# Normalisation ahead of the spread stage: ScalarE scales and writes four of the eight tokens of a tile, VectorE the other four

## The chip, the cores and the metric

The kernel runs on one core of a Trainium2 chip. Its time is the device time of one launch in microseconds (us), lower is better. The profiled execution has its own time, and the profile counts its times from the start of the span that it recorded.

## What is computed

The program is four blocks of an image network on an input of 4 images, 64 channels, 128 x 128 pixels. The change touches only the start of the last convolution-like block (L3): a normalisation over the 64 channels of every pixel, whose result goes into repeated rolls and 3 x 3 depthwise filters.

```python
def _ln_c(v, eps=1e-06):
    m = jnp.mean(v, axis=1, keepdims=True)
    s = jnp.var(v, axis=1, keepdims=True)
    return (v - m) / jnp.sqrt(s + eps)
...
def _L3_conv_ref(x, w_d, w_u, w_r, w_l, bn_d, bn_u, bn_r, bn_l):
    ...
    for w, bn, dil, sign, axis in dirs:
        dim = H if axis == 2 else W
        for i in range(ITER):
            shift = dim // 2 ** (ITER - i)
            idx = (np.arange(dim) + sign * shift) % dim
            xs = x[:, :, idx, :] if axis == 2 else x[:, :, :, idx]
            x = x + ALPHA * jax.nn.relu(_aspp(xs, w[i], bn[i], dil))
    return x
...
x = x + _L3_conv_ref(_ln_c(x), ...)
```

## The kernel before

The stages run one after the other (window attention, a choice layer, a convolution, a top-2 layer, sweeps, a choice layer, spread, a top-2 layer), each with its own semaphores, and every stage ends in a barrier of all engines. `stage_spread` is the one that changes. It has two phases: the normalisation, and then 8 groups of 16 filter steps on TensorE, ScalarE and VectorE. TensorE, ScalarE and VectorE wait for the last tile of the normalisation (L2678, L2656, L2605) before the first filter step, so nothing of the second phase lies beside the first except the building of filter bands on GpSimd and their loads.

A tile of the normalisation is 128 partitions (image rows) x 8 tokens (pixels of a row) x 64 channels, 512 elements in each partition. There are 16 positions t times 4 images b, 64 tiles. For tile n the steps are:

- SP loads the tile into `xs` (L2469), four buffers deep, each load after GpSimd has read the buffer's last tile.
- VectorE sums the channels (`total`, L2587) and divides by 64 (`mean`, L2591).
- GpSimd subtracts the mean into `h` (`center`, L2518), four buffers deep. It waits for the mean, and for the scaled tile four back.
- ScalarE squares `h` (`square`, L2648), VectorE sums the squares (`variance`, L2595), ScalarE takes the root (`root`, L2653).
- VectorE inverts the root (L2600) and multiplies `h` by it into `passes` (`scale`, L2602). `passes` is the array [128, 64 channels, 4 images, 128 columns], so that consecutive channels of one token are written 512 floats (2048 bytes) apart, while `h` is read without gaps. `passes` is read by the filter steps alone.

`pipelined` sets the order on each engine: every step has a lead d, and in step v of the loop the engine does, one after the other, each function for tile v + d. VectorE's list is `[(total, 3), (variance, 1), (mean, 3), (scale, 0)]`, ScalarE's `[(root, 1), (square, 2)]`, GpSimd's `[(center, 3)]`. In VectorE's step v stand the total of tile v + 3, the variance of tile v + 1, the mean of tile v + 3, and the inverse and the scaling of tile v. The loop body holds four steps, with three steps of filling ahead and the last ones written out after it. A counter is raised by 4 at the start where four buffers are free from the beginning (L2510, L2511).

Of the kernel before, what the change touches and what calls it, by code (L numbers as in the profile page):

```python
# [6 lines left out]
ALU = mybir.AluOpType  # L7
ACT = mybir.ActivationFunctionType
AX = mybir.AxisListType
B, C, H, W = 4, 64, 128, 128  # L10
# [64 lines left out]
def bcast(v, n, m=C):  # L75

    return v.unsqueeze(2).to_broadcast([128, n, m])


def pipelined(eng, tiles, stages):  # L80

    def step(v):
        for f, d in stages:
            if 0 <= v + d < B * tiles:
                f((v + d) // B, (v + d) % B, v + d)

    for v in range(-max(d for _, d in stages), B):
        step(v)  # L90
    with eng.Fori(1, tiles - 1) as t:
        for k in range(B):
            for f, d in stages:
                f(t + (k + d) // B, (k + d) % B, B * t + k + d)
    for v in range(B * (tiles - 1), B * tiles - min(d for _, d in stages)):
        step(v)
# [2229 lines left out]
def stage_spread(nc, tok, w_d, w_dirs, bns, y, windows):  # L2326
# [9 lines left out]
    TS = 8  # L2336
    NT = W // TS
# [9 lines left out]
    with ExitStack() as ctx:  # L2347
        a = Arena(nc, ctx, "sp")
# [7 lines left out]
        st = a.sb("st", [128, B, 2, TS])  # L2356

        xs = work[:, 0:2048].rearrange("p (n t c) -> p n t c", n=B, t=TS)
        h = work[:, 2048:4096].rearrange("p (n t c) -> p n t c", n=B, t=TS)
# [23 lines left out]
        inverted = a.sem("inverted")  # L2383
# [2 lines left out]
        var_ready = a.sem("var_ready")  # L2386
        std_ready = a.sem("std_ready")
        y_ready = a.sem("y_ready")
        band_in = [a.sem(f"band_in{i}") for i in range(LOADS)]
        band_ready = a.sem("band_ready")  # L2390
        y_done = a.sem("y_done")
# [12 lines left out]
        def columns(n, b, t):  # L2404

            v = y[:, :, bass.ds(b, 1), bass.ds(TS * t, TS)]
            return v.rearrange("p c a w -> p (a w) c")

        def channel(g, q):
            return y[:, NC * g + q, :, :].rearrange("p b w -> p (b w)")  # L2410

        def place(i, q):

            return x[:, (q, q, 8 + q if q < 4 else q - 4, 4 + q)[i // IT], :]
# [19 lines left out]
        def loads_before(slot, j):  # L2434

            return 16 * sum(2 * len(row_parts(k)) for k in range(j) if k % LOADS == slot)
# [54 lines left out]
        @block.gpsimd  # L2491
        def _(pool):
            link = Link(pool, pool_done)

            pool.memset(eps[:, 0:1], EPS_LN)
            pool.memset(eps[:, 1:2], EPS_BN)
            pool.memset(bands[0:C + 1, :], 0.0).then_inc(vs_clear, 1)
            link(pool.memset(roll[:, :, :], 0.0))

            def set_diagonal(m, c0, c1, k):  # L2500

                link(pool.affine_select(out=m[:, c0:c1], in_=m[:, c0:c1], compare_op=ALU.not_equal, fill=1.0,
                                        base=-c0 - k, pattern=[[-1, c1 - c0]], channel_multiplier=1))

            for i, s in enumerate(SHIFTS):
                for c0 in (0, R):
                    set_diagonal(roll[:, i, :], c0, c0 + R - s // 2, s // 2)
                    set_diagonal(roll[:, i, :], c0 + R - s // 2, c0 + R, s // 2 - R)
            pool.sem_inc(const_ready, 1)
            pool.sem_inc(centered, 4)  # L2510
            pool.sem_inc(y_ready, 4)  # L2511
            pool.sem_inc(var_ready, 2)

            def center(t, b, n):

                pool.wait_ge(mean_ready, n + 1)
                pool.wait_ge(y_ready, n + 1)
                pool.tensor_tensor(h[:, b, :, :], xs[:, b, :, :], bcast(st[:, b, 0, :], TS),  # L2518
                                   ALU.subtract).then_inc(centered, 1)

            pipelined(pool, NT, [(center, 3)])

            def turn_over(g, j):

                pool.wait_ge(band_in[j % LOADS], g * loads_before(j % LOADS, NV) + loads_before(j % LOADS, j + 1))
                last = NV * g + j - BANDS
                if last >= 0:
                    for q in range(NC - 4, NC):
                        pool.wait_ge(conv_ready[q], 2 * (ITS * (last // NV) + IT + last % NV + 1))
                src = hankel[:, j % LOADS, :].rearrange("p (q n) -> p q n", q=NC)[:, :, 0:3 * R]  # L2530
                dst = band[:, (NV * g + j) % BANDS, :, :, :].rearrange("p q k m -> p q (k m)")
                pool.tensor_copy(dst, src[:, :, ::-1]).then_inc(band_ready, 1)  # L2532

            def put_back(g, q):


                pool.wait_ge(x_ready[q], ITS * (g + 1))
                src = place(ITS - 1, q).rearrange("p (b s m k) -> p s b m k", b=B, s=2, m=8)
                dst = channel(g, q).rearrange("p (b m s k) -> p s b m k", b=B, s=2, m=8)
                for here in range(2):  # L2540
                    for there in range(2):
                        ins = pool.tensor_copy(dst[halves[there], here], src[halves[here], there])
                        if here == 0 or there == 0:
                            link(ins)
                ins.then_inc(y_done, 1)
                pool.wait_ge(y_done, NC * g + q + 1)

            for j in range(BANDS):
                turn_over(0, j)
            for g in range(GROUPS):  # L2550
                for j in range(BANDS, NV):
                    turn_over(g, j)
                for q in range(NC):
                    put_back(g, q)
                    if g < GROUPS - 1 and q in (3, 5, 7):
                        turn_over(g + 1, (q - 3) // 2)

        @block.vector
        def _(dve):
# [3 lines left out]
            for d in range(3):  # L2563
                dil = (1, 2, 4)[d]
                for kh in range(3):
# [3 lines left out]
                    ins = dve.tensor_copy(vs[0:C, d, 0:IT, 3, at], w[:, 0:IT, 0])  # L2569
# [22 lines left out]

            def variance(t, b, n):
                dve.wait_ge(squared, n + 1)
                dve.tensor_reduce(st[:, b, 1, :], sq[:, b % 2, :, :], AX.X, ALU.add).then_inc(var_ready, 1)  # L2595

            def scale(t, b, n):
                s = st[:, b, 1, :]
                dve.wait_ge(std_ready, n + 1)
                dve.reciprocal(s, s).then_inc(inverted, 1)  # L2600
                dve.wait_ge(inverted, n + 1)
                dve.tensor_tensor(columns(n, b, t), h[:, b, :, :], bcast(s, TS), ALU.mult).then_inc(y_ready, 1)  # L2602

            pipelined(dve, NT, [(total, 3), (variance, 1), (mean, 3), (scale, 0)])
            dve.wait_ge(y_ready, B * NT + 4)  # L2605

            def add(g, i, q):
                old, new = x_before(g, i, q), place(min(i + 1, ITS - 1), q)
# [29 lines left out]
        @block.scalar  # L2638
        def _(act):
            act.wait_ge(const_ready, 1)  # L2640
            act.wait_ge(p_in, 16 * 5)
            var = raw_bn[:, :, :, 3, :]
            act.activation(var, var, ACT.Sqrt, bias=eps[:, 1:2]).then_inc(bn_std, 1)

            def square(t, b, n):
                act.wait_ge(centered, n + 5)
                act.wait_ge(var_ready, n + 1)
                act.activation(sq[:, b % 2, :, :], h[:, b, :, :], ACT.Square).then_inc(squared, 1)  # L2648

            def root(t, b, n):  # L2650
                s = st[:, b, 1, :]
                act.wait_ge(var_ready, n + 3)
                act.activation(s, s, ACT.Sqrt, bias=eps[:, 0:1], scale=1.0 / C).then_inc(std_ready, 1)  # L2653

            pipelined(act, NT, [(root, 1), (square, 2)])
            act.wait_ge(y_ready, B * NT + 4)  # L2656
            act.wait_ge(par_ready, 1)

            def relu(g, i, q, out, rows_out, rows_in):
                c = NC * g + q  # L2660
                return act.activation(out[rows_out, :], pC[q][rows_in, :], ACT.Relu, bias=par[rows_in, c, BI + i:BI + i + 1],  # L2661
                                      scale=par[rows_in, c, SC + i:SC + i + 1])

            for g in range(GROUPS):
                for i in range(ITS):
                    for q in range(NC):
                        act.wait_ge(conv_ready[q], 2 * (ITS * g + i + 1))
                        if aside(i, q):
                            relu(g, i, q, side[:, q // 4, :], halves[0], halves[1])
                            ins = relu(g, i, q, side[:, q // 4, :], halves[1], halves[0])  # L2670
                        else:
                            ins = relu(g, i, q, pC[q], slice(0, 128), slice(0, 128))
                        ins.then_inc(relu_ready[q], 1)

        @block.tensor
        def _(pe):
            pe.wait_ge(const_ready, 1)
            pe.wait_ge(y_ready, B * NT + 4)  # L2678


            MINUS, MIDDLE, PLUS = range(3)
# [98 lines left out]
```

## Time and profile before

| what | value |
|---|---|
| median of 3 runs | 7505.19 us (7491.1 to 7510.78) |
| the profiled execution's own time | 7501.84 us |
| its span | 7500.1 us |
| granted TensorE clock, mean of the span | 0.853 |
| VectorE busy, all stages | 4316.2 us (58%) |
| ScalarE busy, all stages | 3784.3 us (50%) |
| GpSimd busy, all stages | 1430.9 us (19%) |
| first operation of the normalisation phase | 5012.44 us |
| first matmul after it | 5215.08 us |

The last two rows bound the phase: 203 of 7500 us. The shares of the whole span say little about it, as the other stages have other limits. It has to be read from a timeline of its own stretch, from the durations of its lines, and from what its engines wait for.

### The profile page before, as it was taken

The numbers are of one execution on the slowest core, as the hardware profiler recorded it, in microseconds if no ns is written. First come the engines' busy times: TensorE is split into PE (matmuls) and PEld (weight loads), VectorE is DVE, ScalarE is ACT, GpSimd is POOL, SyncE is SP. The second block draws the span as 40 slices with busy tenths as digits, with TensorE's granted clock in tenths as the row PEclk, the third lists the DMA queues.
The fourth block names the chain that finished last, engine by engine and source line by source line (L and its number), as shares of the span: only waits on it lengthen the run. The fifth ranks groups of instructions, "written<-read, shape, count | busy, mean of one in ns | idle before, by whom it ended". The sixth has DMA issues, their size and how long they took to land. (4 is left out here: it accounts for less than half of the span.)

```text
span 7500.1 us, 128640 instructions
## 1 busy us (share of the span) xinstructions
PE 5733.5 (76%) x43616; PEld 3796.3 (51%) x43616; DVE 4316.2 (58%) x8974; ACT 3784.3 (50%) x7044; POOL 1430.9 (19%) x1334
## 2 busy tenths in 40 slices
PE   6776777666697777669979997541999999566666
PEld 4555556315354333359979994240555555332222
DVE  5665666563622777772223345538777777565565
ACT  5665666542643666462233323403666676454453
POOL 2332333432421000050000002312111121111110
PEclk9888888875698888869989998755999999777778
DMA  0101000121232767530000022214666676256666
GB/s 25 29 23 29 21 26 23 57 68 34 84 87 86 241 233 232 199 91 0 0 0 0 34 101 86 62 51 89 82 84 86 75 85 80 40 178 176 178 178 189
DMA packets 791912, 645.40 MB, mean 86 GB/s; under 512 B 494273, under 2 KB 641921, under 8 KB 791501
## 3 DMA queue, kind: packets, MB, share of 16 engines
q1 hardware_dynamic: 790477, 639.00, 35.0%
q8 instruction: 241, 3.95, 0.2%
q14 instruction: 170, 1.39, 0.1%
q0 software_dynamic: 1024, 1.05, 0.1%
HBM read 549.73 MB, written 90.20 MB: 85 GB/s over the span
## 5 line engine op out<-in xcount | busy, mean ns | idle before, releaser
L2300 PE MATMUL sw_pC<-sw_row,sw_wc 128*128 128x128 f32 x10160 | 1159.2, 274 | 56.8 <-DVE sw_row L2175 54.9
L2300 PEld LDWEIGHTS sw_pC<-sw_row,sw_wc 128*128 128x128 f32 x10160 | 1148.6, 191 | 58.1 <-DVE sw_row L2175 55.5
L2721 PE MATMUL sp_pC<-sp_work,sp_bands 64*64 64x512 f32 (+11 forms) x14592 | 986.1, 428 | 44.7 <-issue 44.7
L2721 PEld LDWEIGHTS sp_pC<-sp_work,sp_bands 64*64 64x64 f32 x14592 | 596.3, 133 | 437.8 <-issue 369.5
L2163 DVE SCALAR_TENSOR_TENSOR sw_row<-sw_pC,sw_y 128x128 f32<-128x128 f32 x1016 | 337.8, 332 | 792.7 <-PE sw_pC L2300 792.7
L2661 ACT ACTIVATE sp_pC<-sp_pC,sp_par 128x512 f32<-128x512 f32 x832 | 597.7, 740 | 375.5 <-PE sp_pC L2721 349.6
L1715 DVE TENSOR_TENSOR t_z<-t_z,t_ht 128x1024 f32<-128x1024 f32 x512 | 601.9, 1233 | 150.2 <-DMA t_z<-gate_rows 149.3
L1874 PE MATMUL t_pO<-t_z,t_ew 128*64 128x512 f32 x2048 | 557.5, 690 | 36.4 <-DVE t_z L1715 35.8
L2232 ACT ACTIVATE sw_y<-sw_row 128x128 f32 (+1 forms) x762 | 265.3, 348 | 593.6 <-DVE sw_row L2163 593.6
L2624 DVE TENSOR_TENSOR sp_work<-sp_work,sp_pC 128x512 f32<-128x512 f32 x512 | 351.0, 687 | 171.2 <-ACT sp_pC L2661 170.7
L1844 PE MATMUL t_pT<-t_ident,t_h 128*128 128x128 f32 x1024 | 195.8, 354 | 274.3 <-ACT t_gs L1771 157.9
L309 POOL TENSOR_TENSOR wa_sc<-wa_sc,wa_sm 128x1024 f32<-128x1024 f32 x128 | 243.3, 1901 | 712.0 <-DVE wa_sm L406 712.0
L1005 PE MATMUL c_pG<-c_ht,c_gate_cols 128*32 128x512 f32 x512 | 291.0, 703 | 80.7 <-ACT c_ht L950 80.7
L579 PE MATMUL wa_pS<-wa_ks,wa_qs 128*128 128x256 f32 x1024 | 322.2, 470 | 23.2 <-issue 18.3
L1874 PEld LDWEIGHTS t_pO<-t_z,t_ew 128*64 128x64 f32 x2048 | 153.0, 159 | 361.0 <-issue 263.1
L1844 PEld LDWEIGHTS t_pT<-t_ident,t_h 128*128 128x128 f32 x1024 | 156.2, 183 | 340.0 <-issue 275.8
L1780 ACT ACTIVATE t_oc<-t_pO 128x512 f32<-128x512 f32 x128 | 76.6, 599 | 497.4 <-PE t_pO L1874 497.4
L579 PEld LDWEIGHTS wa_pS<-wa_ks,wa_qs 128*128 128x128 f32 x1024 | 246.3, 244 | 110.1 <-issue 64.6
L2661 ACT ACTIVATE sp_side<-sp_pC,sp_par 64x512 f32<-64x512 f32 x384 | 297.0, 773 | 7.5
L2532 POOL COPY sp_bands<-sp_bands 128x1536 f32<-128x1536 f32 x96 | 141.4, 1473 | 815.0 <-PE sp_pC L2721 778.0
L393 DVE TENSOR_TENSOR wa_sc<-wa_pS,wa_bias 128x1024 f32<-128x1024 f32 (+1 forms) x128 | 147.8, 1155 | 252.9 <-PE wa_pS L579 250.2
L455 ACT ACTIVATE wa_qs<-wa_pQK,wa_gmask 128x256 f32<-128x256 f32 x256 | 107.3, 470 | 363.4 <-PE wa_pV L572 363.4
(346 smaller groups left out, 10834.3 us busy)
## 6 DMA issues: line engine op xcount, KB each, us to landing
t_z<-gate_rows SPq DMA_DIRECT2D x512, 512.0 KB, 6.7
sp_bands<-windows SPq DMA_DIRECT2D x128, 512.0 KB
c_xs<-tokens SPq DMA_DIRECT2D x128, 256.0 KB, 2.6
cb_xs<-tokens SPq DMA_DIRECT2D x128, 256.0 KB, 2.8
wa_xs<-in_x SPq DMA_DIRECT2D x64, 256.0 KB, 2.9
tokens<-wa_xt SPq DMA_DIRECT2D x128, 128.0 KB, 2.1
tokens<-cb_h SPq DMA_DIRECT2D x64, 256.0 KB, 2.4
t_xs<-tokens SPq DMA_DIRECT2D x32, 512.0 KB, 9.3
```

What stands on the lines that cost most here:

```text
L309: pool.tensor_tensor(p, p, r, ALU.mult).then_inc(probs_ready, 1)
L579: ins = pe.matmul(pS[:, w, :, :], qs[:, w, :, :].rearrange("p g q -> p (g q)"), ks[:, :, 64 * w:64 * w + 64], start=True, stop=True)
L1005: ins = pe.matmul(pG[m][E * b:E * b + E, :], gate_cols[:, m, :], ht[:, b % 2, :], start=True, stop=True)
L1715: dve.tensor_tensor(z[:, i, q, :], z[:, i, q, :], ht[:, m.k % HR, i, :], ALU.mult).then_inc(z_ready, 1)
L1844: ins = pe.transpose(pT[s][:, 128 * j:128 * j + 128], h[:, i, 4 * s + j, :, :].rearrange("p c d -> p (c d)"), ident[:, :])
L1874: ins = pe.matmul(pO[i][64 * s:64 * s + 64, :], ew[:, q, :], z[:, i, q, 512 * s:512 * s + 512], start=(q == 0), stop=(q == 3))
L2163: dve.scalar_tensor_tensor(row[par][c][:, :, PAD:PAD + P2], pC[c][:, 0:2 * P2].rearrange("p (b w) -> p b w", b=2), 0.0, line(sweep, c, i), ...
L2232: act.activation(line(sweep, c, i), row[par][c][:, :, PAD:PAD + P2], ACT.Copy).then_inc(saved[c], 1)
L2300: ins = pe.matmul(pC[c][:, 0:2 * P2], wc[:, sweep, m, :], row[1 - par][c][:, :, m:m + P2], start=(m == 0), stop=(m == 4))
L2624: return dve.tensor_tensor(new, old, rel, ALU.add)
L2661: return act.activation(out[rows_out, :], pC[q][rows_in, :], ACT.Relu, bias=par[rows_in, c, BI + i:BI + i + 1], scale=par[rows_in, c, SC + ...
L2721: ins = pe.matmul(out[halves[to], :, low * lo:low * hi], band[halves[k], (NV * g + j) % BANDS, q, AT[k][tap], :], v[halves[k], :, low * at ...
```

## The change

ScalarE gets a third function in its list, `scale_rest` with lead 0, behind `root` and `square`: after VectorE's inverse of tile n it multiplies tokens 4 to 7 of tile n by their inverse, one ACTIVATE (Copy with a scale read from `st`, one value in each partition) for each token, 128 x 64 elements, and writes them into `passes`. VectorE's multiplication now covers tokens 0 to 3. A new semaphore `rest_ready` counts tiles whose second half is written: GpSimd waits for it before it writes `h` again, VectorE before it writes the variance again (`st` is read by ScalarE until then), and TensorE and VectorE wait for the last tile's second half before the filter steps.

```diff
@@ stage_spread, GpSimd @@
+            pool.sem_inc(rest_ready, 4)
...
                 pool.wait_ge(mean_ready, n + 1)
                 pool.wait_ge(y_ready, n + 1)
+                pool.wait_ge(rest_ready, n + 1)
                 pool.tensor_tensor(h[:, b, :, :], xs[:, b, :, :], bcast(st[:, b, 0, :], TS),
@@ VectorE @@
             def variance(t, b, n):
                 dve.wait_ge(squared, n + 1)
+                dve.wait_ge(rest_ready, n + 1)
...
-                dve.tensor_tensor(columns(n, b, t), h[:, b, :, :], bcast(s, TS), ALU.mult).then_inc(y_ready, 1)
+                dve.tensor_tensor(columns(n, b, t)[:, 0:TS // 2, :], h[:, b, 0:TS // 2, :], bcast(s[:, 0:TS // 2], TS // 2),
+                                  ALU.mult).then_inc(y_ready, 1)
...
             dve.wait_ge(y_ready, B * NT + 4)
+            dve.wait_ge(rest_ready, B * NT + 4)
@@ ScalarE @@
-            pipelined(act, NT, [(root, 1), (square, 2)])
+            def scale_rest(t, b, n):
+                act.wait_ge(inverted, n + 1)
+                for k in range(TS // 2, TS):
+                    ins = act.activation(columns(n, b, t)[:, k, :], h[:, b, k, :], ACT.Copy, scale=st[:, b, 1, k:k + 1])
+                ins.then_inc(rest_ready, 1)
+
+            pipelined(act, NT, [(root, 1), (square, 2), (scale_rest, 0)])
@@ TensorE @@
             pe.wait_ge(y_ready, B * NT + 4)
+            pe.wait_ge(rest_ready, B * NT + 4)
```

How the order on ScalarE changes, at the first step of the loop body. Before (ISA and REGISTER_ALU rows work out addresses and counts):

```order
L91 ISA
L2653 ACTIVATE sp_st<-sp_st,sp_eps 128x8
L2646 REGISTER_ALU
L2647 REGISTER_ALU
L2648 ACTIVATE sp_work<-sp_work 128x512
```

The changed kernel's ScalarE at the same place (L2659 is the root, L2654 the square, L2664 the new line):

```order
L91 ISA
L2659 ACTIVATE sp_st<-sp_st,sp_eps 128x8
L2652 REGISTER_ALU
L2653 REGISTER_ALU
L2654 ACTIVATE sp_work<-sp_work 128x512
L2662 REGISTER_ALU
L2664 ISA
L2664 ACTIVATE passes<-sp_work,sp_st 128x64
L2664 ISA
L2664 ACTIVATE passes<-sp_work,sp_st 128x64
```

Two more such pairs follow for the last two tokens; then comes the next step's root. No table load stands between them. VectorE before, from the variance of the first step in the loop body to its scaling:

```order
L2595 TENSOR_REDUCE sp_st<-sp_work 128x8
L2590 REGISTER_ALU
L2591 TENSOR_SCALAR sp_st<-sp_st 128x8
L2599 REGISTER_ALU
L2600 RECIPROCAL sp_st<-sp_st 128x8
L2602 ISA
L2602 TENSOR_TENSOR passes<-sp_work,sp_st 128x8x64
```

VectorE of the changed kernel at the same place:

```order
L2599 TENSOR_REDUCE sp_st<-sp_work 128x8
L2593 REGISTER_ALU
L2594 TENSOR_SCALAR sp_st<-sp_st 128x8
L2603 REGISTER_ALU
L2604 RECIPROCAL sp_st<-sp_st 128x8
L2606 ISA
L2606 TENSOR_TENSOR passes<-sp_work,sp_st 128x4x64
```

The rows and their order stay; the multiplication has half the elements.

## Rows read from the trace of the kernel before

**Rows 1.** The page: span, and busy time of each engine.
```profile
span 7500.1 us, 128640 instructions
PE 5733.5 (76%) x43616; PEld 3796.3 (51%) x43616; DVE 4316.2 (58%) x8974; ACT 3784.3 (50%) x7044; POOL 1430.9 (19%) x1334
```

**Rows 2.** Waits of TensorE: who waited for whom, us in total, times, longest.
```profile
PE sp_pC L2734 <- DVE passes L2602: 246.2, 1, 246.2
```

**Rows 3.** Groups by line, 5016.0 to 5209.3: busy us, mean ns | idle before.
```profile
L2602 DVE TENSOR_TENSOR passes<-sp_work,sp_st 128x512 f32 (+1 forms) x61 | 107.3, 1758 | 8.2
...
L2653 ACT ACTIVATE sp_st<-sp_st,sp_eps 128x8 f32<-128x8 f32 x62 | 18.7, 301 | 142.9 <-DVE sp_st L2595 142.9
```

**Rows 4.** Timeline of one step: start us, us, engine, line, operation [idle before].
```profile
5103.10 0.15 DVE L2591 TENSOR_SCALAR sp_st<-sp_st 128x8 f32<-128x8 f32 x1
5103.17 0.19 DVE L2600 RECIPROCAL sp_st<-sp_st 128x8 f32<-128x8 f32 x1
5103.21 0.30 ACT L2653 ACTIVATE sp_st<-sp_st,sp_eps 128x8 f32<-128x8 f32 x1 [2.36 <-DVE sp_st L2595]
5103.33 1.04 POOL L2518 TENSOR_TENSOR sp_work<-sp_work,sp_st 128x512 f32<-128x512 f32 x1 [2.13 <-DVE sp_st L2591]
5103.42 0.61 ACT L2648 ACTIVATE sp_work<-sp_work 128x512 f32<-128x512 f32 x1
5103.50 1.75 DVE L2602 TENSOR_TENSOR passes<-sp_work,sp_st 128x512 f32 x1
...
5105.10 0.66 DVE L2587 TENSOR_REDUCE sp_st<-sp_work 128x8 f32<-128x512 f32 x1
...
5106.28 0.15 DVE L2591 TENSOR_SCALAR sp_st<-sp_st 128x8 f32<-128x8 f32 x1
```

**Rows 5.** Durations of three lines: ns min/median/max, first and last start.
```profile
L2602 DVE TENSOR_TENSOR passes<-sp_work,sp_st x64: 1011/1749/1861, 5017.6 to 5213.9; 128x512 f32 x56, 128x512 f32<-128x512 f32 x8
...
L878 DVE TENSOR_TENSOR c_h<-c_h,c_st x64: 691/1528/1566, 1413.5 to 4801.2; 128x512 f32<-128x512 f32 x64
...
L1653 DVE TENSOR_TENSOR t_rw<-t_rw,t_z x2: 167/168/169, 2409.1 to 6494.5; 128x8 f32<-128x8 f32 x2
```

**Rows 6.** Timeline of another stage's normalisation.
```profile
4602.64 1.04 POOL L830 TENSOR_TENSOR c_h<-c_xs,c_st 128x512 f32<-128x512 f32 x1 [4.20 <-DVE c_st L866]
4602.70 1.53 DVE L878 TENSOR_TENSOR c_h<-c_h,c_st 128x512 f32<-128x512 f32 x1
```

**Rows 7.** Timeline of the end of the phase.
```profile
5210.86 0.61 ACT L2648 ACTIVATE sp_work<-sp_work 128x512 f32<-128x512 f32 x1
5212.05 0.66 DVE L2595 TENSOR_REDUCE sp_st<-sp_work 128x8 f32<-128x512 f32 x1
...
5213.92 1.01 DVE L2602 TENSOR_TENSOR passes<-sp_work,sp_st 128x512 f32<-128x512 f32 x1
```

**Rows 8.** Durations of ScalarE lines in other stages, as in rows 5.
```profile
L1347 ACT ACTIVATE cb_xb<-cb_zero x8: 239/240/240, 1997.5 to 2376.0; 128x64 f32<-128x64 f32 x8
...
L1787 ACT ACTIVATE t_y<-t_pY x64: 576/578/599, 2470.7 to 3144.9; 128x512 f32<-128x512 f32 x64
L1787 ACT ACTIVATE passes<-t_pY x64: 1009/1016/1074, 6590.7 to 7479.1; 128x512 f32 x48, 128x512 f32<-128x512 f32 x16
...
L1753 ACT ACTIVATE t_h<-passes,t_nm,t_sd x512: 451/484/508, 6520.4 to 7435.0; 128x126 f32 x128, 128x126 f32<-128x126 f32 x43
```

**Rows 9.** Timeline of ScalarE: eight activations of L1753 in a row.
```profile
6623.25 3.15 ACT L1753 ACTIVATE t_h<-passes,t_nm,t_sd 128x126 f32 x8
```

**Rows 10.** Timeline: ScalarE writes `passes`, and VectorE beside it.
```profile
6622.43 1.02 ACT L1787 ACTIVATE passes<-t_pY 128x512 f32<-128x512 f32 x1
...
6623.03 0.23 DVE L1705 TENSOR_TENSOR t_one<-t_one,t_ex 128x128 f32<-128x128 f32 x1
```

**Rows 11.** SP's loads of tiles: issue ns, and time to landing.
```profile
L2469 SPq DMA_DIRECT2D sp_work<-tokens x128: 598/607/1927, 4998.4 to 5197.5; - x128
...
DMA to landing us min/median/max: 2.6/2.8/6.4
```

More of the change, by code:

```diff
@@ L2388, in stage_spread @@
         y_ready = a.sem("y_ready")
+        rest_ready = a.sem("rest_ready")
         band_in = [a.sem(f"band_in{i}") for i in range(LOADS)]
```

## The prediction

> **What bounds the kernel now.** I read the page first, for where the stage lies: the engines' shares over all stages [rows 1] say nothing about a phase of 203 us. What matters for it is TensorE's waits: its longest single one, 246.2 us, ends with the last write of `passes` by L2602 [rows 2]. So the whole second phase stands behind the normalisation, and a microsecond saved there should come off the total one for one, if the filter steps then take what they take now.
>
> Next the groups by line in the steady part [rows 3]. In 193.3 us VectorE's L2602 alone is busy 107.3 us with only 8.2 us of idle ahead of it, while ScalarE sat 142.9 us waiting for the variance. VectorE is the engine without a gap. The timeline of one step shows why it is [rows 4]: the mean starts at 5103.10, the next step's at 5106.28, a pitch of 3.18 us, and between them VectorE does the inverse, the scaling (1.75 us), and then the total at 5105.10, 0.15 us before the scaling's recorded end.
>
> The 1.75 us is not the price of 512 elements. The same line takes 1.01 us at its shortest [rows 5], at the very end of the phase [rows 7], where center is over. In the step, GpSimd's center runs from 5103.33 to 5104.37, starting 0.17 us ahead of the scaling, and the scaling ends at 5105.25, 0.88 us after it [rows 4]. VectorE does next to nothing of it until GpSimd is through. Another stage has the same picture with a write without gaps: center ends at 4603.68, the multiplication at 4604.23, 0.55 us later [rows 6], where free it takes 0.69 us [rows 5]. The Trainium skill (SBUF — State Buffer, "Who interferes with whom") says that a VectorE instruction with two SBUF inputs contends with a GpSimd instruction that reads SBUF, as an exclusive lock for the whole instruction. By that rule the trace agrees: 1.75 us beside center, 1.01 us without.
>
> **The change part by part.**
>
> *Half of the scaling leaves VectorE.* Only the tail behind center shrinks; the locked 0.87 us stays. The tail is 0.88 us for 512 elements into strided places and 0.55 us into places without gaps; the difference, 0.33 us, grows with the elements, and so do most of the 0.55 us: a multiplication of 8 elements takes 168 ns and one of 512 takes 691 [rows 5], 1.04 ns an element, so 512 elements are 0.53 of the 0.55. The tail is then about 0.015 + 512 x 1.68 ns, and 256 elements leave 0.445 us. Saved: 0.43 us a step. Bounds: a tail wholly in proportion gives 0.44; if the 0.14 us by which a free one is longer than its tail (1.01 - 0.88) also stands in the tail, half is 0.51 and the step saves 0.37. I take 0.43, since the small multiplication places the fixed part outside the tail. What is late next is the same chain, center then the shorter tail: 5104.37 + 0.445 - 0.15 puts the next total at 5104.67 instead of 5105.10, a pitch of 2.75 us.
>
> The step with the tail occurs 61 times: L2602 from its first start at 5017.6 to the end of the steady part at 5209.3 [rows 3, 5]. 61 x 0.43 = 26.2 us.
>
> *Four activations go to ScalarE.* No row shows a 128 x 64 activation with a scale pointer into strided places. Lower bound: 0.24 us, a plain 128 x 64 copy; upper bound 0.48 us, 126 elements with a bias and a scale pointer [rows 8]. In between: 0.24, plus 64 x (1016 - 578)/512 ns = 0.055 for the stride, plus a pointer. The 484 ns of L1753 are 240 + 62 elements at some 0.8 ns + two pointers, so about 0.097 each. That is 0.39 us. Eight L1753 in a row take 3.15 us [rows 9], (3.15 - 0.48)/7 = 0.38 apart where each lasts 0.48, so neighbours overlap by 0.10; the pitch P of the new ones is 0.29, and of the bounds 0.14 and 0.38. The register work between them is inside L1753's pitch as well. The Trainium skill (ScalarE: Activation LUTs, "What ACT_TABLE_LOAD costs") prices an ACTIVATE at 186 ns + 0.833 ns an element, 93 ns for a pointer, with 93 ns of overlap: an estimate from that page is 0.33 us without the stride, a pitch of 0.24, and the sum below would be the same by it.
>
> ScalarE's step is then root 0.21 + square 0.52 (starts at 5103.21 and 5103.42, its 0.61 less the overlap) + 4 x 0.29 = 1.9 us, against a pitch of 2.75. With the upper P it is 2.25. It starts with the variance and ends at about 5105.2, before the next root at 5105.96 and before the next center at 5106.08, the first that waits for it. Cost on the path: nothing. The cover is VectorE's pitch, and it is gone at P = 0.50.
>
> *The new waits.* Center's on `rest_ready`: 0.9 us of slack as worked out, with nothing queued behind on GpSimd but the next center. The variance's on `rest_ready`: for a tile three steps back, long done; the sequencer meets it while the total runs, and behind it are the variance, the mean and the scaling. I price both at nothing; no row shows such a wait by itself, and the nearest step, 0.07 us from one short instruction to the next [rows 4], would give 61 x 0.07 = 4.3 us as the upper bound. Below nothing there is no room: a wait does no work.
>
> *Loads.* SP needs two issues of 0.61 us a tile and 2.8 us to landing [rows 11]; from the end of center to the total four steps on there are 4 x 2.75 - 2.4 = 8.6 us. No cost.
>
> *The end of the phase.* Here the gain is not had. VectorE's last three scalings would end 1.3 us earlier against the steady part. But ScalarE must still write three halves: its square ends at 5211.47 [rows 7], the first four follow until 5212.6; the root of the last tile (variance at 5212.05, 0.43 sooner, done by 5212.3) until 5212.8; four until 5213.9; four more until 5215.2 with the last one's full length. Now the last scaling ends at 5214.93. So the end is 0.25 us later than now, on top of the 26.2.
>
> **Sum.** 26.2 - 0.25 = 26.0 us. Against the profiled execution's own 7501.84 (span 7500.1) that gives 7475.9. That execution is 3.35 us under the median of the runs, so I forecast for the median 7505.19 - 26.0 = 7479.2, as **7479 us**, a gain of 0.35%. The likeliest case's own size runs from 61 x 0.37 - 0.25 = 22.3, or 18 with the upper price of the waits, to 61 x 0.44 = 26.8 us; the three runs lie 20 us apart, so 7467 to 7491.
>
> **The rivals.**
>
> *Two strided writers get in each other's way, gain gone.* In the new step VectorE's tail (5104.37 to 5104.81) lies in the middle of ScalarE's writes (5103.9 to 5105.2) into the same array. If each then runs at half speed, the tail of 0.445 doubles to 0.89 and VectorE's pitch is what it is now: 7505. Against it: ScalarE writes `passes` for 1.02 us while L1705, a two-input VectorE instruction, takes its usual 0.23 us [rows 10]; but that one writes without gaps, so it doesn't settle it. For it: both engines pay for the stride by a like amount (0.6 and 0.86 ns an element), which could be one limit at the memory. The skill's SBUF page, in the section named above, says that ScalarE never waits on anyone for SBUF; no run here shows two strided writers together.
>
> *ScalarE becomes the bound, slower than before.* The same collision, felt by ScalarE. Its step is 0.73 + 4P; at P = 0.50 it takes over from VectorE, and from P = 0.61 the step is longer than today's 3.18. If each of the four lasts twice its 0.39, P is 0.68 and the step 3.45: 61 x 0.27 = 16 us slower, 7522. Center, the variance and the root would all wait for it. Against it: even the dearest short row has P = 0.38.
>
> *The tail does not shrink.* If the 0.88 us were mostly a handing over after GpSimd, and not elements, half the elements would save little: 7505. Against it: the tails of 0.88 and 0.55 for equal counts differ exactly as the free durations do.
>
> **How the numbers follow.** About 0.3% (22.5 us) is what a measurement of this kernel tells from no change. Main case 0.76; collision with the gain gone or mostly gone 0.12; ScalarE as the bound 0.05; tail that stays 0.07. Of the main case about seven tenths come out beyond 22.5 us (forecast 26, sizes down to 18, and medians that move by some us), the rest within. Faster: 0.76 x 0.71 + 0.01 = 0.55. Slower: 0.05 and a little for drawn runs, 0.06. Same: 0.39. The range reaches from a little under the main case's lower end, 7465, to the no-gain cases at 7505; outside stay the slower case and the tails of the runs.
>
> **What would show it.** Right: L2602's successor (L2606) at 1.25 to 1.35 us in the steady part, its end 0.43 to 0.46 after center's; pitch of the means 2.75; L2664 near 0.39 us; TensorE's wait shorter by 26 us; ScalarE still waiting for the variance, some 0.85 us a step. Wrong: a tail of 0.6 us or more (collision, or a fixed part); L2664 over 0.6 us; center waiting for ScalarE instead of for the mean; or a phase shorter by 26 us and a total that is not, which would put the loss into the filter steps or the top-2 stage behind them.

## The result, and the profile after

The changed kernel takes 7472.21 us (median of 8 runs, 7463.21 to 7491.64), the kernel before 7502.62 us (median of 8, 7491.1 to 7511.44). The ratio is 0.9963 with a 95% interval of 0.9950 to 0.9975, a gain of 28 us (19 to 38); the two medians themselves lie 30.4 us apart. The forecast was 7479 us and a gain of 26.0 us, 0.35%, with a range of 7465 to 7505: the time lies inside it, and the interval of the gain holds the forecast. The gain is just over the 0.3% that the prediction called measurable, so the totals alone would not tell 26 us from 20 or from 35.

The wait in which TensorE stands before the filter steps shows the change without the noise of the other stages. It was 246.2 us [rows 2]. Now (waits of TensorE: who waited for whom, us in total, times, longest):

```profile
PE sp_pC L2747 <- ACT passes L2664: 220.1, 1, 220.1
```

That is 26.1 us less, where 26.0 was forecast, and the releaser is now ScalarE's last activation instead of VectorE's last multiplication, as the forecast's end of the phase had it.

The groups by line in the steady part of the changed kernel, against [rows 3] (busy us, mean ns | idle before):

```profile
L2606 DVE TENSOR_TENSOR passes<-sp_work,sp_st 128x256 f32 (+1 forms) x61 | 81.1, 1330 | 8.2
L2664 ACT ACTIVATE passes<-sp_work,sp_st 128x64 f32 (+1 forms) x243 | 67.0, 387 | 0.0
...
L2659 ACT ACTIVATE sp_st<-sp_st,sp_eps 128x8 f32<-128x8 f32 x61 | 18.3, 301 | 55.9 <-DVE sp_st L2599 55.9
```

VectorE's multiplication went from 1.76 to 1.33 us on the mean, though it has half the elements. ScalarE took 67 us of new work and still waits 55.9 us for the variance, in place of 142.9. One step of the timeline, against [rows 4]:

```profile
5103.14 0.16 DVE L2594 TENSOR_SCALAR sp_st<-sp_st 128x8 f32<-128x8 f32 x1
5103.21 0.19 DVE L2604 RECIPROCAL sp_st<-sp_st 128x8 f32<-128x8 f32 x1
5103.25 0.30 ACT L2659 ACTIVATE sp_st<-sp_st,sp_eps 128x8 f32<-128x8 f32 x1 [0.92 <-DVE sp_st L2599]
5103.37 1.04 POOL L2521 TENSOR_TENSOR sp_work<-sp_work,sp_st 128x512 f32<-128x512 f32 x1 [1.71 <-DVE sp_st L2594]
5103.46 0.61 ACT L2654 ACTIVATE sp_work<-sp_work 128x512 f32<-128x512 f32 x1
5103.54 1.32 DVE L2606 TENSOR_TENSOR passes<-sp_work,sp_st 128x256 f32 x1
5103.98 1.10 ACT L2664 ACTIVATE passes<-sp_work,sp_st 128x64 f32 x4
5104.71 0.66 DVE L2590 TENSOR_REDUCE sp_st<-sp_work 128x8 f32<-128x512 f32 x1
...
5105.89 0.16 DVE L2594 TENSOR_SCALAR sp_st<-sp_st 128x8 f32<-128x8 f32 x1
```

The means are 2.75 us apart (3.18 before). Center ends at 5104.41 and the multiplication at 5104.86, 0.45 us later (0.88 before). The first 0.87 us of the multiplication, beside center, are still there: they are two thirds of VectorE's instruction. ScalarE's four activations end at 5105.08, well before the next root at 5106.00.

The end of the phase in the changed kernel, against [rows 7]:

```profile
5200.11 1.46 POOL L2535 COPY sp_bands<-sp_bands 128x1536 f32<-128x1536 f32 x1 [2.25 <-DMA sp_bands<-windows]
...
5200.53 1.49 DVE L2606 TENSOR_TENSOR passes<-sp_work,sp_st 128x256 f32<-128x256 f32 x1
5200.72 1.11 ACT L2664 ACTIVATE passes<-sp_work,sp_st 128x64 f32<-128x64 f32 x4
5201.86 0.18 DVE L2604 RECIPROCAL sp_st<-sp_st 128x8 f32<-128x8 f32 x1
5202.08 0.59 DVE L2606 TENSOR_TENSOR passes<-sp_work,sp_st 128x256 f32<-128x256 f32 x1
5202.08 1.12 ACT L2664 ACTIVATE passes<-sp_work,sp_st 128x64 f32<-128x64 f32 x4 [0.25 <-DVE sp_st L2604]
```

The last tile's activations end at 5203.20, 0.5 us after VectorE's last one. The size came out as forecast, but not all of the way there: the band copy on GpSimd, which now waits for its load, falls on VectorE's multiplication of the last tile but one (1.49 us where free it takes 0.59; in the kernel before it fell one tile earlier, on a multiplication of 1.44 us where free it takes 1.01), and ScalarE waits 0.25 us for the last inverse. The forecast had ScalarE busy without a gap there.

The two profiled executions differ by 19.6 us of span (7500.1 and 7480.5), which is not the phase's 26.1. TensorE's first matmul after the wait starts at 5215.08 in one and 5203.34 in the other, 11.7 us earlier, so the stages ahead of the phase, whose code is the same, took 14.4 us longer in the second execution; what follows the phase took 7.9 us less. Single executions scatter by that much, so a change of this size is better read in its own wait than in one total.

### The profile page after: what moved, and what is told of

Same layout as the page of the kernel before. It is cut to its first block and busy times, and to the rows that moved or that the text cites. A ratio compares the mean times of both kernels' runs of the same rounds, so it can differ in the third digit from the quotient of the medians.

```text
span 7480.5 us, 129214 instructions
## 1 busy us (share of the span) xinstructions
PE 5739.0 (77%) x43616; PEld 3804.1 (51%) x43616; DVE 4287.6 (57%) x8974; ACT 3848.5 (51%) x7300; POOL 1433.9 (19%) x1334
```

## Experiments

Each kernel ran beside the kernel before on the same chip. Of each I read two things: the ratio of the times, and TensorE's wait, which carries the phase without the rest.

### The tail by the number of elements: VectorE six tokens, or two

```diff
-                dve.tensor_tensor(columns(n, b, t)[:, 0:TS // 2, :], h[:, b, 0:TS // 2, :], bcast(s[:, 0:TS // 2], TS // 2),
+                dve.tensor_tensor(columns(n, b, t)[:, 0:6, :], h[:, b, 0:6, :], bcast(s[:, 0:6], 6),
...
-                for k in range(TS // 2, TS):
+                for k in range(6, TS):
```

> VectorE scales tokens 0 to 5 of a tile, ScalarE 6 and 7. Elements theory (the tail behind center is 0.015 us + 1.68 ns an element): the 384 elements of VectorE leave a tail of 0.66 us, the scaling lasts 1.53 to 1.55 us, the step is 2.96 us, TensorE's wait is 246.2 - 61 x 0.215 = 233 us, the ratio to the kernel before 0.998. Fixed-part theory (0.14 us of the tail belongs to the handing over): the half's 0.445 us then would not lie on this line, and 384 elements leave 0.69 us or more, a step of 3.0 us. Collision theory (two strided writers slow each other): fewer strided writes on ScalarE, so the tail is shorter than 0.66 us.

Measured: 7498.59 against 7509.36 us, ratio 0.9984 (0.9975 to 0.9994). TensorE's wait and one step:

```profile
PE sp_pC L2747 <- DVE passes L2606: 232.6, 1, 232.6
```
```profile
5093.36 1.04 POOL L2521 TENSOR_TENSOR sp_work<-sp_work,sp_st 128x512 f32<-128x512 f32 x1 [1.92 <-DVE sp_st L2594]
...
5093.53 1.54 DVE L2606 TENSOR_TENSOR passes<-sp_work,sp_st 128x384 f32 x1
```

Center ends at 5094.40, the multiplication at 5095.07: a tail of 0.67 (0.66 as the median of the 61). The step is 2.96 us as forecast, and TensorE's wait 232.6 us for 233.

The same edit with 2 for 6:

> VectorE scales tokens 0 and 1 of a tile, ScalarE 2 to 7. Elements theory: a tail of 0.23 us for 128 elements, a step of 2.53 us; ScalarE's step is 0.73 + 6 x 0.24 = 2.2 us and stays below it, so VectorE still bounds. TensorE's wait is 220.1 - 61 x 0.215 = 207 us, plus 1 to 2 us at the end of the phase, where ScalarE writes the last three tiles' six tokens after one another: 208 to 209. The ratio to the kernel before is 0.995. Fixed-part theory: a tail of 0.30 us or more and a wait of 213 us. Collision theory: ScalarE's strided writes now cover the whole tail and the step, its activations last over 0.45 us, and the step is 2.75 us or more.

Measured: 7473.67 against 7509.36 us, ratio 0.9942 (0.9924 to 0.9961).

```profile
PE sp_pC L2747 <- ACT passes L2664: 208.6, 1, 208.6
```
```profile
5091.49 1.04 POOL L2521 TENSOR_TENSOR sp_work<-sp_work,sp_st 128x512 f32<-128x512 f32 x1 [1.49 <-DVE sp_st L2594]
...
5091.66 1.14 DVE L2606 TENSOR_TENSOR passes<-sp_work,sp_st 128x128 f32 x1
```

The four tails, medians over 61 steps, are 0.875 us for 512 elements, 0.66 for 384, 0.447 for 256 and 0.266 for 128. The first three lie on a line of 1.67 ns an element with 0.02 us left at zero; the last is 0.04 longer than the line, but the step is not (2.536 us for 2.53). The third rival of the prediction, a tail that does not shrink, is out. So is the collision of two strided writers in the size that the prediction gave it, a tail or an activation of twice the length: in the changed kernel ScalarE's activations cover the whole tail, and it lies on the line. Here, with six activations, ScalarE writes for 1.6 of every 2.5 us, and the step is as short as elements alone make it (durations of ScalarE's activations in ns min/median/max, in the changed kernel and in this one).

```profile
L2664 ACT ACTIVATE passes<-sp_work,sp_st x256: 383/387/402, 5032.5 to 5202.8; 128x64 f32 x112, 128x64 f32<-128x64 f32 x16
```
```profile
L2664 ACT ACTIVATE passes<-sp_work,sp_st x332: 383/387/427, 5039.7 to 5179.5; 128x64 f32 x165, 128x64 f32<-128x64 f32 x1
```

In the changed kernel the activation lasts 387 ns whether it meets VectorE's tail or not. In this one the maximum is 427, and it is no stray: the second of the six activations, the one for token 3, lasts over 395 ns in 60 of 64 tiles (0.423 us as a median), the other five last 387.

```profile
5092.33 0.42 ACT L2664 ACTIVATE passes<-sp_work,sp_st 128x64 f32 x1
```

It lies across VectorE's tail (5092.53 to 5092.80), and its 0.036 us are the size of what that tail has too much. So there is a small collision here, and it costs nothing, as the step shows. The rule that the prediction took from the Trainium skill (SBUF — State Buffer, "Who interferes with whom"), that ScalarE never waits on anyone, agrees with the 387 ns of the changed kernel, but not with these 423, and here the measurement decides. What makes the difference is not shown; the last section says what these activations have in common.

### ScalarE's part alone

VectorE multiplies all eight tokens; ScalarE makes its four activations as well, into a scratch buffer without gaps.

```diff
+        flat = a.sb("flat", [128, B, TS // 2, C])
...
-                dve.tensor_tensor(columns(n, b, t)[:, 0:TS // 2, :], h[:, b, 0:TS // 2, :], bcast(s[:, 0:TS // 2], TS // 2),
-                                  ALU.mult).then_inc(y_ready, 1)
+                dve.tensor_tensor(columns(n, b, t), h[:, b, :, :], bcast(s, TS), ALU.mult).then_inc(y_ready, 1)
...
+                act.wait_ge(rest_ready, n + 1)
                 for k in range(TS // 2, TS):
-                    ins = act.activation(columns(n, b, t)[:, k, :], h[:, b, k, :], ACT.Copy, scale=st[:, b, 1, k:k + 1])
+                    ins = act.activation(flat[:, b, k - TS // 2, :], h[:, b, k, :], ACT.Copy, scale=st[:, b, 1, k:k + 1])
```

> Only ScalarE's part of the change: VectorE multiplies all eight tokens as before, and ScalarE makes its four activations all the same, with the new waits, but into a scratch buffer without gaps that nobody reads. Hidden theory (the four activations and the waits cost nothing while VectorE's step is the longer one): step 3.18 us, scaling 1.75 us, TensorE's wait 246 to 247 us, ratio 1.000; the activations last about 0.33 us, and their pitch shows whether the stride costs time between them (0.24 us with it in the changed kernel). Waits theory: up to 0.07 us a step, TensorE's wait 250 us.

Measured: 7508.17 against 7509.36 us, ratio 1.0002 (0.9993 to 1.0012).

```profile
PE sp_pC L2748 <- ACT sp_flat L2665: 246.7, 1, 246.7
```
```profile
L2665 ACT ACTIVATE sp_flat<-sp_work,sp_st x177: 331/332/335, 5039.8 to 5179.8; 128x64 f32<-128x64 f32 x177
```

The activations and all the new waits together cost 0.5 us on the phase, some 0.3 of it over the 61 steps and the rest at the end. The step is 3.183 us on the mean, 3.178 in the kernel before. The waits theory's 250 us is out. The activation lasts 332 ns without the stride and 387 with it, but starts follow each other after 0.24 us in both: the stride costs time in an activation, not time between activations.

### The lock: the scaling ahead of the mean

The kernel before, with one list reordered. Nothing goes to ScalarE.

```diff
-            pipelined(dve, NT, [(total, 3), (variance, 1), (mean, 3), (scale, 0)])
+            pipelined(dve, NT, [(total, 3), (variance, 1), (scale, 0), (mean, 3)])
```

> The kernel before with one edit: in VectorE's list the scaling stands ahead of the mean, so that center, which waits for the mean, starts after the scaling and runs beside the total and the variance, which have one input from SBUF. ScalarE has no part of the scaling. Lock theory (the 0.74 us between 1.75 and 1.01 is time in which GpSimd's center keeps VectorE's two-input instruction out): the scaling lasts 1.01 us, the step is 0.58 + 0.60 + 0.33 + 0.86 + 0.07 = 2.44 us, TensorE's wait 246.2 - 61 x 0.74 = 201 us, the ratio 0.994. Rival (the scaling is slow in the steady part for another reason, such as the loads landing beside it or ScalarE's square): 1.75 us and 246 us as before.

Measured: 7462.68 against 7509.36 us, ratio 0.9935 (0.9921 to 0.9949). TensorE's wait and a step:

```profile
PE sp_pC L2734 <- DVE passes L2602: 201.8, 1, 201.8
```
```profile
5091.54 1.03 DVE L2602 TENSOR_TENSOR passes<-sp_work,sp_st 128x512 f32 x1
5092.41 0.16 DVE L2591 TENSOR_SCALAR sp_st<-sp_st 128x8 f32<-128x8 f32 x1
5092.47 0.68 DVE L2587 TENSOR_REDUCE sp_st<-sp_work 128x8 f32<-128x512 f32 x1
5092.67 1.04 POOL L2518 TENSOR_TENSOR sp_work<-sp_work,sp_st 128x512 f32<-128x512 f32 x1 [1.42 <-DVE sp_st L2591]
5093.07 0.68 DVE L2595 TENSOR_REDUCE sp_st<-sp_work 128x8 f32<-128x512 f32 x1
...
5094.00 1.03 DVE L2602 TENSOR_TENSOR passes<-sp_work,sp_st 128x512 f32 x1
```

Center now lies beside the total and the variance, which take 0.68 us each (0.66 and 0.67 before). The scaling, with all 512 elements, the loads and ScalarE's square beside it, takes 1.03 us for 1.75, and the step 2.46 us for the 2.44 expected. So the 0.72 us were center's, and the rival (loads, or the square) is out. This one reordered list saves 44 us, more than the change under study.

### Both edits

> Both edits: the changed kernel (ScalarE scales four of eight tokens) with VectorE's list reordered, the scaling ahead of the mean. Lock and elements theory: the scaling of 256 elements is free of center and lasts 0.59 us, VectorE's step is order_full's 2.46 - 0.43 = 2.03 us, ScalarE's 0.73 + 4 x 0.24 = 1.7 us stays below it; TensorE's wait is 201.8 - 61 x 0.43 = 176 us, plus 0.3 to 2 us at the end of the phase for ScalarE's last tokens; the ratio to the kernel before is 0.991. Rival, a new bound at this pitch: SP needs two issues and some register work for a tile (1.65 us in the kernel before) and a landing 2.8 us later, so the total may begin to wait for its load; VectorE would then show idle time released by the DMA, the step would be 2.2 us or more and the wait 187 us or more.

Measured: 7436.28 against 7511.88 us, ratio 0.9904 (0.9887 to 0.9920).

```profile
PE sp_pC L2747 <- ACT passes L2664: 175.9, 1, 175.9
```

```profile
5090.11 0.60 DVE L2606 TENSOR_TENSOR passes<-sp_work,sp_st 128x256 f32 x1
...
5092.14 0.59 DVE L2606 TENSOR_TENSOR passes<-sp_work,sp_st 128x256 f32 x1
```

The step is 2.03 us. The two gains add: 44.4 for the order and 25.9 for the split. The loads did not become the bound; VectorE shows no wait for a load in 110 us of the steady part, and SP itself waited 13.0 us for center there (49.9 in the kernel before over the same stretch).

With six tokens on VectorE:

> As order_split, but VectorE scales six tokens and ScalarE two. Lock and elements theory: scaling 0.80 us, step 2.46 - 0.22 = 2.24 us, TensorE's wait 188 to 190 us. Rival of order_split (loads): here nearly nothing is lost to them, so that the two kernels differ by less than 61 x 0.21 = 13 us.

Measured: 7454.26 against 7511.88 us, ratio 0.9928 (0.9911 to 0.9944).

```profile
PE sp_pC L2747 <- DVE passes L2606: 188.5, 1, 188.5
```

The step is 2.24 us as expected, with a scaling of 0.83 us for 0.80. TensorE's wait is 12.6 us longer than with four and four, which is too near the 13 us to exclude the rival by itself; the steps do, as they differ by 0.215 us, the whole price of two tokens. The rest is at the end of the phase, where this kernel's ScalarE has less left to write.

### ScalarE made the bound

The prediction's second rival was not met in the changed kernel. With the lock gone it can be brought about, by giving ScalarE six tokens (`0:2` and `range(2, TS)`) in the reordered kernel:

> As order_split, but VectorE scales two tokens and ScalarE six, so that ScalarE should be the bound: the prediction's second rival, brought about. VectorE alone would need 2.03 - 2 x 0.107 = 1.81 us a step. ScalarE-bound theory: its step is 0.73 + 6 x 0.24 = 2.17 us, ScalarE shows hardly a wait, VectorE waits for it, and TensorE's wait is 246.2 - 61 x 1.01 = 185 us plus 1 to 2 us at the end: slower than order_split (175.9) although VectorE has less to do. Rival (VectorE still bounds): 1.81 us a step and a wait of 163 us.

Measured: 7439.08 against 7509.51 us, ratio 0.9905 (0.9889 to 0.9922).

```profile
PE sp_pC L2747 <- ACT passes L2664: 184.9, 1, 184.9
```
```profile
5091.59 1.04 POOL L2521 TENSOR_TENSOR sp_work<-sp_work,sp_st 128x512 f32<-128x512 f32 x1 [1.10 <-ACT passes L2664]
5091.99 1.58 ACT L2664 ACTIVATE passes<-sp_work,sp_st 128x64 f32 x6
5092.11 0.69 DVE L2599 TENSOR_REDUCE sp_st<-sp_work 128x8 f32<-128x512 f32 x1 [0.24 <-ACT sp_work L2654]
```

The step is 2.14 us, ScalarE's own 0.73 + 6 x 0.24 = 2.17 within 0.03. Center waits for ScalarE's writes, no longer for the mean, and VectorE waits for the square. The phase is 9 us longer than with four tokens each, though VectorE has half as much to multiply; in the total this is within the noise.

Between the two, three tokens on VectorE and five on ScalarE:

> As order_split, but VectorE scales three tokens and ScalarE five: both engines should need 1.92 us a step. If they mesh without a gap, TensorE's wait is 175.9 - 61 x 0.11 = 169 us plus 0.5 at the end; if ScalarE's waits for the variance (0.20 us a step in order_split) stay, its step is 2.1 us and the wait 181 us, no better than order_split. In time to order_split no difference of over 0.1% is expected.

Measured: 7431.03 against 7509.51 us, ratio 0.9893 (0.9876 to 0.9909).

```profile
PE sp_pC L2747 <- ACT passes L2664: 171.8, 1, 171.8
```

The step is 1.92 us as a median and 1.95 as a mean, since the last of the loop's four takes 2.04 at the branch back. The engines mesh; the wait is 4 us shorter than with four and four. By the total the two cannot be told apart. This kernel has the shortest wait and the lowest median of all, 1.1% under the kernel before.

## Why the prediction was right, point by point

**What bounds the phase.** Right. VectorE had hardly a gap (8.2 us in 193), TensorE's wait carried the gain, and in every experiment what the wait lost lies inside the interval of the ratio: from 246.2 to 175.9 us are 70 us, and a ratio of 0.9904 takes 72 off 7511.88. That the total's gain of 28 us came so near 26.0 is in part luck, as its interval is 19 us wide; the 26.1 us of the wait are the better witness.

**The locked stretch.** Read from the shortest duration, the tail after center and another stage's like pair, and shown by order_full: 1.75 us becomes 1.03 when center lies elsewhere. The prediction used this only to price the half; it did not say that the lock could be taken away, for more than the change brings.

**The tail.** 0.445 us forecast, 0.447 measured; 61 x 0.43 = 26.2 of the 26.1 us. The choice between the bounds (0.37 and 0.44 saved) by the small multiplication was right: the first three sizes leave a fixed part of 0.02 us. A size taken from one point and an argument was enough here because two free durations and two tails agreed.

**The activations.** The duration was right, 0.387 us for 0.39. Their pitch P was sized too high: 0.29 forecast, 0.24 measured. The step that failed is the sum of base price, stride and pointer less an overlap of 0.10 taken from activations whose pitch that overlap described. With the stride the overlap is 0.15: the 0.055 us for the stride stand in the duration only. The estimate that the prediction drew from the Trainium skill (ScalarE: Activation LUTs, "What ACT_TABLE_LOAD costs"), 0.33 us and a pitch of 0.24 without the stride, is what the flat ones show (0.332 and 0.24), and the strided ones have the same pitch. The miss in P changed nothing in the sum, as the cover was wide (1.7 us of 2.75).

**The new waits.** Nothing, as priced: at most 0.005 us a step in the kernel with ScalarE's part alone. Their upper bound of 4.3 us widened the range for nothing.

**The end of the phase.** A loss of 0.25 us against the steady part was forecast, and about 0.1 came (61 steps of 0.429 us are 26.2, and 26.1 were measured in all), by another way than worked out: ScalarE was quicker than forecast, and the band copy on GpSimd took part of it back by holding VectorE's multiplication of the last tile but one. That these two nearly cancel is luck.

**The rivals.** None came about in the changed kernel. The tail that stays is excluded by the runs with two and six tokens, and the collision by the changed kernel's own tail and activations, which lie beside each other and have their forecast lengths. A collision of a tenth of an activation appears with VectorE on two tokens, far from the doubling that the prediction priced. ScalarE as the bound is real, but only past the point that the prediction named (its step over VectorE's).

## What to carry to other kernels

Before work is moved off the engine that bounds a loop, take its longest instruction apart into its own time and the time in which another engine keeps it out: compare its shortest duration with its usual one, and look for a constant distance to the end of a neighbour's instruction. Here the split of the scaling shortened only the part behind GpSimd and gained 26 us, while the exchange of two entries in an order list, so that GpSimd's subtraction lies beside sums with one input, gained 44 us without any work moved. With that done, the split still gave its full 26, and the division with the shortest wait was the one in which the two engines' steps are equal (here 3 to 5), each step being a sum of starts that the trace shows. Against four and four that was 4 us of the wait, too little for the total to show.

## What the runs showed of the hardware

An activation of 128 x 64 elements with a scale pointer takes 332 ns when its output is without gaps and 387 when its elements are 2048 bytes apart, yet in both cases the next one starts 0.24 us later. I had expected the stride to be paid in the pitch.

VectorE's and ScalarE's writes 2048 bytes apart into the same array, at the same time, did not slow each other with four tokens each: 387 ns for the activation, and 0.447 us for VectorE's 256 elements behind center, about half of the 0.875 us that 512 take without a neighbour.

In two kernels they did, by little. With VectorE on tokens 0 and 1, ScalarE's activation for token 3 takes 423 ns where it lies beside VectorE's writes, and the one for token 4, beside them too, takes 387. With VectorE on tokens 0 to 5 and the order changed, the activation for token 6 takes over 395 ns in 43 of 64 tiles; it starts while VectorE's scaling still runs. Common to both is that the two engines then write tokens of the same group of four, 16 bytes in a row (2 and 3 beside 0 and 1, 6 and 7 beside 4 and 5), which four and four never do. That this is the cause is a guess; no run tests it.
